# ScalarE's normalisation and routing pieces moved from the end of a pair slot into its middle, in a one-core attention and mixture-of-experts kernel

## The chip, the cores and the metric

The kernel runs on one core of a Trainium2 chip. The metric is the device time of one execution in microseconds (us). Before the change the median of three runs is 1081.94 us (1081.14 to 1083.57).

## What is computed

The input is x, 8 batches of 512 tokens with 128 features, and a conditioning vector per batch. Cut to what matters:

```python
h = layernorm(x) * (1 + ca) + sa
x = x + ga * attention(h, W_qkv, W_out)        # 16 heads of 64, rotary, causal mask, softmax
h = layernorm(x) * (1 + cb) + sb
x = x + gb * moe(h)                            # 8 experts, top 2, gelu, then a layernorm and + h
```

The router takes the two largest of eight logits, the expert's input rows are gathered by expert, and the residual inside the expert block is added afterwards.

## The kernel before, in words

**Stages.** A short opening (some 30 us) loads the data and prepares batches 0 and 1. Then comes the attention stage, which lasts to about 810 us and also does the routing of each finished batch. After it come the last routing pieces, the expert stage and a closing stage.

**The attention stage is a hand-written pipeline.** A *pair* is two heads of one batch; there are 64 of them, 8 per batch. The stage is a loop over 68 *slots*, numbered by step i (0 to 8) and c (0 to 7); slot (i, c) is number 8i + c. In one slot the engines work on three pairs at once: q0, whose q and k are projected, rotated and rounded to a high and a low part; q1, whose scores are computed, masked and exponentiated; and q2, whose exponentials are finished and transposed, multiplied with the values and projected. Every engine has its own instruction queue, written out in a fixed order by `pe_slot`, `act_slot`, `dve_slot`, `pool_slot` and `sp_slot` (lines 950 to 1218), and waits on semaphores for the others. Each engine starts a slot when it has finished the one before.

**TensorE's order in a slot** (`pe_slot`, line 950): the six projection matmuls of q0 (lines 852 to 859), the transposes "0" and "2a" of q2 (line 915), the scores of q1 of tile row 3 (lines 889 to 894), further transposes, the values of q2 (line 937), transposes "3a" of q1, more scores, the output projection of q2 (line 946), transposes "3b", the value projection (lines 873 to 875), then in slots c = 0, 2, 4, 6, 7 a routing or normalisation piece in PSUM bank 6, then the last scores. `pe_scores` of tile row 3 has to wait for the sixth exponential of q2 (unit 5), because that frees its PSUM banks:

```python
if due(NU * n + 2 * idx - 2):
    e.wait_ge(a_exp, NU * n + 2 * idx - 2)
```

**ScalarE's order in a slot** (`act_slot`, line 1043): exponentials 5, 6, 7 of q2; copies of transposes "0" and "2a"; `act_rep`; copy of "1"; `act_r`; exponentials 0 to 3 of q1 (line 996, the first waits for VectorE's maximum, `nmax`); the copy of "3a"; `act_hi` twice (line 1024, the rounding of k and of q, each of which waits for GpSimd's sum at line 1173); `act_v` (line 1028); exponential 4 of q1; and at the very end `route_act`. So what `route_act` does stands between exponential 4 and exponential 5 of the same pair.

**The side work** of step i belongs to other batches than the attention of that step:

- `n_rows`, `n_turn`, `n_features`, `n_rest` prepare batch i + 2 (steps 0 to 5): normalise the four token tiles of 128 x 128 (line 559), transpose them on TensorE (line 566), shift and scale into `ht2` (line 573) and round to `h_hi` (line 576) on ScalarE, and take the low part `h_lo` on GpSimd (line 581).
- `r_norm`, `r_features`, `r_shift` normalise the finished batch i - 1 (line 288, four tiles), transpose (line 295) and shift (line 303). The factors for it come from GpSimd's `r_factors` at the end of slot 5.
- `r_exp` (line 350), `r_rows` (line 314) and VectorE's `r_one` and others route batch i - 2.

Before the change ScalarE has `r_exp` at the end of slot 1, `r_rows` at the end of slot 2, `n_rows` at the end of slot 3, `n_features` with the rounding at the end of slot 4, `r_norm` at the end of slot 6 and `r_shift` at the end of slot 7. GpSimd takes `n_rest` at the start of slot 5, and waits there for the rounding.

**GpSimd's order in a slot** (`pool_slot`, line 1180): `route_rest`, `route_cum`, `pool_wo`, a wait for VectorE's `ot` of q2 (not in slot 0), `pool_qk` twice, `pool_lo` twice, `route_pool`. `pool_qk` also waits for four small transfers on SP's queue, which swap the halves of the heads for the rotation (line 1199). The first SP issue of a slot waits for VectorE's product at line 1075.

The side work that is left at the end of the 68 slots is walked through in `LATE` (line 1329), slots (8, 4) to (10, 1), with no attention beside it.

Of the kernel before, what the change touches and what calls it, by code (L numbers as in the profile page):

```python
# [13 lines left out]
B, S, E = 8, 512, 128  # L14
NT = B * S // P
TB = S // P
# [7 lines left out]
FIRST = 2  # L24
# [18 lines left out]
def due(value):  # L43

    return not isinstance(value, int) or value > 0
# [13 lines left out]
def adaln_kernel(nc, x_in, w_qkv, w_out, gate_w, expert_bias, w_up, w_down, c_t, w_mod,  # L59
                 cos_in, sin_in, ident_in, tri_in, rank_in, const_in, out, xs, ys):  # L60
    ctx = ExitStack()
    with ctx:
# [215 lines left out]
            e.wait_ge(r_rs, b + 1)  # L278
            e.tensor_tensor(minus, less, rstd4, op=ALU.mult).then_inc(r_fac, 1)

        def r_norm(e, b):
            e.wait_ge(r_fac, b + 1)
            if due(b - 1):
                e.wait_ge(d_xs, 16 * 2 * TB * (b - 1))
                e.wait_ge(d_h2, 16 * (b - 1))
            e.wait_ge(n_tr, min(b + 2, B - FIRST))
            for t in range(TB):
                ins = e.activation(rows[b % 2][:, t, 0:E], x_all[:, b * TB + t, :], ACT.Identity, bias=f4[:, 5, t:t + 1],
                                   scale=f4[:, 4, t:t + 1])
            ins.then_inc(r_xh, 1)  # L290

        def r_features(e, b):
            e.wait_ge(r_xh, b + 1)
# [184 lines left out]
        def route_pe(e, i, c):  # L478
# [9 lines left out]
            if c == 7 and a is not None:  # L488
                r_features(e, a)

        def route_act(e, i, c):
            b, a = batch(i, 2), batch(i, 1)
            if c == 1 and b is not None:
                r_exp(e, b)
            if c == 2 and b is not None:
                r_rows(e, b)
            if c == 3 and coming(i) is not None:
                n_rows(e, i, coming(i))
            if c == 4 and coming(i) is not None:
                n_features(e, i, coming(i))  # L500
            if c == 6 and a is not None:
                r_norm(e, a)
            if c == 7 and a is not None:
                r_shift(e, a)

# [43 lines left out]
            e.scalar_tensor_tensor(out=minus1[:, n], in0=mean[:, n], scalar=-1.0, in1=rstd[:, n],  # L549
                                   op0=ALU.mult, op1=ALU.mult).then_inc(n_fac, 1)  # L550

        def n_rows(e, i, b):
            e.wait_ge(n_fac, 1)
            if due(i - 2):
                e.wait_ge(d_xs, 16 * 2 * TB * (i - 2))
                e.wait_ge(d_h2, 16 * (i - 2))
            for t in range(TB):
                m = b * TB + t
                ins = e.activation(rows[(i + 1) % 2][:, t, 0:E], x_all[:, m, :], ACT.Identity,
                                   bias=minus1[:, m:m + 1], scale=rstd[:, m:m + 1])  # L560
            ins.then_inc(n_xh, 1)

        def n_turn(e, i):
            e.wait_ge(n_xh, i + 1)
# [4 lines left out]
        def n_features(e, i, b):  # L569
            e.wait_ge(n_tr, i + 1)  # L570
            if due(i - 1):
                e.wait_ge(p_x2, i - 1)
            e.activation(ht2[:], ps[:, BANK_R, :], ACT.Identity, bias=mod1[:, 0, b:b + 1],
                         scale=mod1[:, 1, b:b + 1]).then_inc(n_ht, 1)
            e.wait_ge(n_ht, i + 1)
            e.copy(h_hi[:, b * S:(b + 1) * S], ht2[:]).then_inc(n_hi, 1)

# [3 lines left out]
            e.tensor_tensor(h_lo[:, cols], ht2[:], h_hi[:, cols], op=ALU.subtract).then_inc(n_lo, 1)  # L581

        def route_rest(e, i, c):
            if c == 5 and coming(i) is not None:
                n_rest(e, i, coming(i))

        def route_cum(e, i, c):
# [207 lines left out]
        with ExitStack() as ph:  # L795
# [247 lines left out]
            def act_slot(e, i, c):  # L1043
                (q0, q1, q2), v = pairs(i, c), Tile(8 * i + c)
                if q2.live:
                    act_exp(e, q2, 5)
                    act_exp(e, q2, 6)
                    act_exp(e, q2, 7)
                    act_store(e, q2, "0")
                    act_store(e, q2, "2a")  # L1050
                    act_rep(e, q2)
                    act_store(e, q2, "1")
                    act_r(e, q2)
                if q1.live:
                    act_exp(e, q1, 0)
                    act_exp(e, q1, 1)
                    act_exp(e, q1, 2)
                    act_exp(e, q1, 3)
                    act_store(e, q1, "3a")
                if q0.live:  # L1060
                    act_hi(e, q0, 1)
                    act_hi(e, q0, 0)
                if v.live:
                    act_v(e, v)
                if q1.live:
                    act_exp(e, q1, 4)
                route_act(e, i, c)
# [111 lines left out]

            def pool_slot(e, i, c):  # L1180
                q0, _, q2 = pairs(i, c)
                route_rest(e, i, c)
                route_cum(e, i, c)
                if q2.live:
                    pool_wo(e, q2)
                if q0.live:
                    if q2.live and i and c:

                        e.wait_ge(v_ot, q2.n + 1)
                    pool_qk(e, q0, 1)  # L1190
                    pool_qk(e, q0, 0)
                    pool_lo(e, q0, 1)
                    pool_lo(e, q0, 0)
                route_pool(e, i, c)

            def sp_turn(e, q):
# [65 lines left out]
        with ExitStack() as ph:  # L1262
# [194 lines left out]
            with nc.Block() as block:  # L1457
# [50 lines left out]
                def _(e):  # L1508
                    high(e, 0)
                    high(e, 1)  # L1510
                    for i, c in LATE:
                        route_act(e, i, c)
                        if (i, c) == (B + 1, 0):
                            e.wait_ge(s_gb, 1)
                            e.copy(gb[:].rearrange("p b f -> p (b f)"),
                                   ps[:, 0:2, :].rearrange("p b f -> p (b f)")).then_inc(s_gbc, 1)
# [212 lines left out]
```

## Time and profile before

| | |
|---|---|
| median of three runs | 1081.94 us |
| the profiled execution's own time | 1080.8 us |
| its span, first to last instruction | 1078.9 us |
| busy: TensorE / VectorE / ScalarE / GpSimd | 86% / 79% / 68% / 52% of the span |
| mean granted TensorE clock | 0.953 |

The span is cut into stretches by the start of the k projection of each slot (line 852), which TensorE issues first in every slot; what is called "the stretch of slot (i, c)" runs from there to the next such start. In a timeline a row gives the start, the duration, the engine, line and operation, and in brackets how long the engine had been idle before and what released it. Rows of ScalarE overlap by about 0.1 us where one follows the other at once, so the distance of starts is the time that an instruction takes of the queue.

### The profile page before, as it was taken

The page shows a single profiled execution, that of the slowest core. Times are in us where ns is not written, and L with a number is a line of the kernel's source. Part 1 is how long each engine was busy: PE and PEld are TensorE (multiplying, and loading weights), DVE is VectorE, ACT ScalarE, POOL GpSimd, SP SyncE. Part 2 cuts the span into 40 slices and gives each one's busy share as a digit, 9 for nine tenths or more (in the row PEclk, how much of TensorE's full clock was granted, in tenths as well). Part 3 has the DMA queues.
Part 4 walks back from the last instruction along what each step waited for, and adds up shares of the span by engine and source line. Part 5 has one row for each costly group of instructions (what it writes and reads, how often), then busy time and mean ns, then how long its engine had stood idle before and what let it go on. Part 6 is the DMA issues. An engine that isn't in the chain of part 4 may idle for free. (4 is left out here: it accounts for less than half of the span.)

```text
span 1078.9 us, 20269 instructions
## 1 busy us (share of the span) xinstructions
PE 927.0 (86%) x6154; PEld 666.3 (62%) x6154; DVE 847.5 (79%) x1731; ACT 730.2 (68%) x1927; POOL 557.8 (52%) x634
## 2 busy tenths in 40 slices
PE   4599999999999999999999999999996179999800
PEld 2366666666666667667666667666664167888600
DVE  5478888788878888888888888788876569988627
ACT  2278777778777777877777777777774256667504
POOL 1245446444665557465556646564673606766610
PEclk9999999999999999999999999999998579999955
DMA  7222322232222222222322232223122756676334
GB/s 241 53 50 50 74 50 50 50 73 61 50 64 72 60 64 69 60 53 73 79 50 50 64 85 57 56 74 77 45 60 97 237 195 244 244 238 236 126 104 130
DMA packets 67227, 104.27 MB, mean 97 GB/s; under 512 B 11115, under 2 KB 49912, under 8 KB 63536
## 3 DMA queue, kind: packets, MB, share of 16 engines
q1 hardware_dynamic: 59056, 90.53, 29.2%
q0 software_dynamic: 4992, 8.94, 2.8%
q10 hardware_dynamic: 3072, 3.51, 0.9%
q8 instruction: 52, 0.85, 0.3%
q14 instruction: 55, 0.45, 0.1%
HBM read 21.09 MB, written 15.50 MB: 34 GB/s over the span
## 5 line engine op out<-in xcount | busy, mean ns | idle before, releaser
L1173 POOL TENSOR_TENSOR four<-four 128x512 f32<-128x512 f32 x128 | 161.2, 1281 | 334.5 <-DVE ot L1119 213.8
L996 ACT ACTIVATE prob<-ps,nmax 128x512 f32<-128x512 f32 (+3 forms) x512 | 264.5, 529 | 76.1 <-DVE nmax L1096 76.1
L1096 DVE TENSOR_REDUCE nmax<-ps 128x2 f32<-128x1024 f32 (+3 forms) x256 | 211.0, 824 | 8.8
L915 PE MATMUL ps<-ident,prob 128*128 128x128 f32 x1280 | 191.4, 279 | 12.2 <-ACT probt L1017 6.9
L915 PEld LDWEIGHTS ps<-ident,prob 128*128 128x128 f32 x1280 | 142.2, 141 | 62.5 <-ACT prob L996 36.7
L1177 POOL TENSOR_TENSOR qk_lo<-four,qk_hi 128x512 fp32r<-128x512 f32 x128 | 162.3, 1291 | 0.0
L937 PE MATMUL ps<-probt,val 128*64 128x512 f32 (+3 forms) x1024 | 153.6, 442 | 0.2 <-ACT probt L1017 0.2
L1089 DVE TENSOR_TENSOR ps<-ps,tri 128x256 f32<-128x256 f32 x256 | 109.3, 427 | 53.5 <-PE ps L894 52.7
L1024 ACT CAST qk_hi<-four 128x512 fp32r<-128x512 f32 x128 | 79.5, 621 | 96.7 <-POOL four L1173 96.7
L1017 ACT COPY probt<-ps 128x512 f32<-128x512 f32 (+2 forms) x256 | 124.7, 520 | 19.6 <-PE ps L915 19.6
L1585 POOL DMA_INDIRECT results<-y,to_i x92 | 96.6, 1050 | 73.0 <-DVE y L1429 50.7
L889 PE MATMUL ps<-qk_hi 64*128 64x512 f32 (+3 forms) x256 | 105.0, 410 | 17.3 <-ACT prob L996 16.5
L937 PEld LDWEIGHTS ps<-probt,val 128*64 128x64 f32 x1024 | 68.3, 137 | 74.8 <-issue 60.6
L1075 DVE TENSOR_TENSOR four<-ps,turn_s 128x1024 f32<-128x1024 f32 x64 | 78.4, 1224 | 42.7 <-PE ps L859 42.7
L890 PE MATMUL ps<-qk_hi 64*128 64x512 f32 (+3 forms) x256 | 105.6, 413 | 0.0
L996 ACT ACTIVATION_READ_ACCUMULATOR prob<-ps,nmax 128x1 f32 x512 | 105.0, 205 | 0.0
L889 PEld LDWEIGHTS ps<-qk_hi 64*128 64x128 f32 x256 | 47.2, 185 | 66.6 <-issue 54.6
L1526 ACT ACTIVATE hf<-ps 128x512 f32<-128x512 f32 x92 | 55.2, 601 | 45.5 <-PE ps L1373 45.1
L894 PE MATMUL ps<-qk_lo,qk_hi 64*128 64x512 f32 (+3 forms) x256 | 82.1, 321 | 0.0
L892 PE MATMUL ps<-qk_hi,qk_lo 64*128 64x512 f32 (+3 forms) x256 | 82.0, 320 | 0.0
L893 PE MATMUL ps<-qk_lo,qk_hi 64*128 64x512 f32 (+3 forms) x256 | 82.0, 320 | 0.0
L891 PE MATMUL ps<-qk_hi,qk_lo 64*128 64x512 f32 (+3 forms) x256 | 82.0, 320 | 0.0
(222 smaller groups left out, 2163.4 us busy)
## 6 DMA issues: line engine op xcount, KB each, us to landing
four<-four SPq DMA_DIRECT2D x256, 128.0 KB
wt<-wall SPq DMA_DIRECT2D x23, 1024.0 KB, 4.8
xg<-slots SPq DMA_DIRECT2D x23, 288.0 KB, 3.8
hb<-h_hi SPq DMA_DIRECT2D x64, 64.0 KB, 2.1
hb<-h_lo SPq DMA_DIRECT2D x64, 64.0 KB, 2.0
y<-results SPq DMA_DIRECT2D x8, 512.0 KB, 7.3
x_all<-in_x SPq DMA_DIRECT2D x4, 512.0 KB, 10.6
h_hi<-rows SPq DMA_DIRECT2D x8, 256.0 KB, 2.7
```

Of the source, the lines that this page charges most:

```text
L889: e.matmul(o0, hi[top_, 0, cols], hi[top_, 1, 0:w], start=True, stop=False)
L890: e.matmul(o1, hi[low_, 0, cols], hi[low_, 1, 0:w], start=True, stop=False)
L894: e.matmul(o1, hi[low_, 0, cols], lo[low_, 1, 0:w], start=False, stop=True).then_inc(p_s, 1)
L915: mm = e.transpose(ps[:, PT + at % 2, at_block * P:(at_block + 1) * P], prob[:, unit, kk * P:(kk + 1) * P], ident[:])
L937: mm = e.matmul(ps[j * HD:(j + 1) * HD, W0, kk * P:S], v[:, kk, first + j * HD:first + (j + 1) * HD], probt[q.par][:, j, kk, kk * P:S], st ...
L996: e.activation(prob[:, unit, 0:w], ps[:, bank_s(idx) + j, 0:w], ACT.Exp, bias=nmax[:, q.par, idx, j:j + 1], accum_out=den[:, q.par, 2 * i ...
L1017: e.copy(dst, src).then_inc(a_ev, 1)
L1089: e.tensor_tensor(block_, block_, tri[:].unsqueeze(1).to_broadcast([P, 2, P]), op=ALU.add).then_inc(v_tri, 1)
L1096: e.tensor_reduce(nmax[:, q.par, idx, :], ps[:, bank:bank + 2, 0:w], AX.X, ALU.max, negate=True).then_inc(v_max, 1)
L1173: e.tensor_tensor(qk[:, cols], tt[:, cols], ur[:, cols], op=ALU.add).then_inc(g_qk, 1)
L1177: e.tensor_tensor(qk_lo[q.par][:, half, :], qk[:, half * S:(half + 1) * S], qk_hi[q.par][:, half, :], op=ALU.subtract).then_inc(g_lo, 1)
L1585: e.indirect_dma_start(ys, bass.IndirectOffsetOnAxis(to_i[:, j % 4, t:t + 1], 0), y4[:, j % 2, t, :], None, bounds_check=2 * B * S - 1, oo ...
```

## The change

The pieces that read no PSUM bank are taken out of `route_act` into a new `route_act_part(e, i, c, half)`, called twice in a ScalarE slot: with half 0 in front of the first exponential of q1, and with half 1 behind the copy of "3a" and in front of `act_hi`. `r_norm` and `n_rows` do two tiles in each half, and stand a slot later than before (slots 7 and 4). `r_exp` goes from the end of slot 1 to half 0 of slot 2. The rounding to `h_hi` is parted from `n_features` as `n_high` and goes from the end of slot 4 to half 0 of slot 5. GpSimd's `n_rest` goes from the start of slot 5 to slot 6, behind `pool_lo`. `r_rows`, the shift of `n_features` and `r_shift` stay at the end of slots 2, 4 and 7. TensorE's, VectorE's and SP's orders are as before.

```diff
-        def r_norm(e, b):
-            e.wait_ge(r_fac, b + 1)
-            if due(b - 1):
-                e.wait_ge(d_xs, 16 * 2 * TB * (b - 1))
-                e.wait_ge(d_h2, 16 * (b - 1))
-            e.wait_ge(n_tr, min(b + 2, B - FIRST))
-            for t in range(TB):
+        def r_norm(e, b, half):
+            if half == 0:
+                e.wait_ge(r_fac, b + 1)
+                if due(b - 1):
+                    e.wait_ge(d_xs, 16 * 2 * TB * (b - 1))
+                    e.wait_ge(d_h2, 16 * (b - 1))
+                e.wait_ge(n_tr, min(b + 2, B - FIRST))
+            for t in range(2 * half, 2 * half + 2):
                 ins = e.activation(rows[b % 2][:, t, 0:E], x_all[:, b * TB + t, :], ACT.Identity, bias=f4[:, 5, t:t + 1],
                                    scale=f4[:, 4, t:t + 1])
-            ins.then_inc(r_xh, 1)
+            if half:
+                ins.then_inc(r_xh, 1)
...
+        def route_act_part(e, i, c, half):
+
+            b, a = batch(i, 2), batch(i, 1)
+            if c == 2 and half == 0 and b is not None:
+                r_exp(e, b)
+            if c == 4 and coming(i) is not None:
+                n_rows(e, i, coming(i), half)
+            if c == 5 and half == 0 and coming(i) is not None:
+                n_high(e, i, coming(i))
+            if c == 7 and a is not None:
+                r_norm(e, a, half)
+
         def route_act(e, i, c):
             b, a = batch(i, 2), batch(i, 1)
-            if c == 1 and b is not None:
-                r_exp(e, b)
             if c == 2 and b is not None:
                 r_rows(e, b)
-            if c == 3 and coming(i) is not None:
-                n_rows(e, i, coming(i))
             if c == 4 and coming(i) is not None:
                 n_features(e, i, coming(i))
-            if c == 6 and a is not None:
-                r_norm(e, a)
             if c == 7 and a is not None:
                 r_shift(e, a)
...
             e.activation(ht2[:], ps[:, BANK_R, :], ACT.Identity, bias=mod1[:, 0, b:b + 1],
                          scale=mod1[:, 1, b:b + 1]).then_inc(n_ht, 1)
+
+        def n_high(e, i, b):
             e.wait_ge(n_ht, i + 1)
             e.copy(h_hi[:, b * S:(b + 1) * S], ht2[:]).then_inc(n_hi, 1)
...
         def route_rest(e, i, c):
-            if c == 5 and coming(i) is not None:
+            if c == 6 and coming(i) is not None:
                 n_rest(e, i, coming(i))
...
                     act_r(e, q2)
+                route_act_part(e, i, c, 0)
                 if q1.live:
                     act_exp(e, q1, 0)
                     act_exp(e, q1, 1)
                     act_exp(e, q1, 2)
                     act_exp(e, q1, 3)
                     act_store(e, q1, "3a")
+                route_act_part(e, i, c, 1)
                 if q0.live:
                     act_hi(e, q0, 1)
                     act_hi(e, q0, 0)
...
             def pool_slot(e, i, c):
                 q0, _, q2 = pairs(i, c)
-                route_rest(e, i, c)
                 route_cum(e, i, c)
...
                     pool_lo(e, q0, 0)
+                route_rest(e, i, c)
                 route_pool(e, i, c)
```

`n_rows` is split in the same way as `r_norm`, and in the `LATE` loop both halves of `route_act_part` stand in front of `route_act`.

## Rows read from the trace of the kernel before

**Rows 1.** The page, part 2: busy tenths of TensorE in 40 equal slices

```profile
PE   4599999999999999999999999999996179999800
```

**Rows 2.** Busy time by stretch: slots (4, 1) and (6, 4), no piece ahead of them

```profile
core 0: us, PE busy (x) PEld busy (x) DVE busy (x) ACT busy (x) POOL busy (x), PEclk, DMA share, GB/s
640.18:651.50 11.32, 11.32 (x83) 7.84 (x81) 10.13 (x20) 8.63 (x26) 5.42 (x6) 1.00 0.25 60
...
408.93:420.21 11.28, 11.28 (x84) 7.91 (x82) 9.88 (x18) 8.41 (x25) 7.96 (x9) 1.00 0.30 80
```

**Rows 3.** The same view: slot 4 behind n_rows, step 4, and six steps' sum

```profile
443.72:457.01 13.29, 11.88 (x88) 8.40 (x86) 10.23 (x20) 10.74 (x32) 6.02 (x6) 1.00 0.22 51
...
sum 79.26, PE 71.50 PEld 50.35 DVE 60.84 ACT 64.38 POOL 35.09; mean PE 11.92 PEld 8.39 DVE 10.14 ACT 10.73 POOL 5.85
```

**Rows 4.** The same view: slot 5 behind n_features, step 4, and six steps' sum

```profile
457.01:469.07 12.06, 11.43 (x84) 7.93 (x82) 10.37 (x20) 9.31 (x27) 6.09 (x7) 1.00 0.23 54
...
sum 72.27, PE 68.60 PEld 47.63 DVE 61.48 ACT 55.13 POOL 35.71; mean PE 11.43 PEld 7.94 DVE 10.25 ACT 9.19 POOL 5.95
```

**Rows 5.** The same view: slot 7 behind r_norm, step 3, and seven steps' sum

```profile
383.54:396.64 13.10, 11.86 (x88) 8.43 (x86) 10.23 (x19) 10.47 (x30) 5.75 (x6) 1.00 0.22 51
...
sum 93.37, PE 83.60 PEld 58.84 DVE 71.99 ACT 74.66 POOL 41.77; mean PE 11.94 PEld 8.41 DVE 10.28 ACT 10.67 POOL 5.97
```

**Rows 6.** The same view: slots (4, 0) behind r_shift, (4, 3) behind r_rows

```profile
396.64:408.93 12.29, 12.15 (x92) 8.88 (x90) 9.90 (x17) 9.42 (x28) 7.63 (x8) 1.00 0.23 67
...
432.06:443.72 11.66, 11.48 (x83) 7.80 (x81) 10.29 (x21) 8.97 (x26) 5.29 (x6) 1.00 0.32 80
```

**Rows 7.** Timeline of TensorE in slot (3, 7)

```profile
386.77 0.46 PE L889 MATMUL ps<-qk_hi 64*128 64x512 f32 x1 [1.04 <-ACT prob L996]
...
395.56 0.60 PE L295 MATMUL ps<-ident,rows 128*128 128x128 f32 x4
396.09 0.38 PE L889 MATMUL ps<-qk_hi 64*128 64x256 f32 x1
```

**Rows 8.** Timeline of ScalarE in slot (3, 7) and the start of (4, 0)

```profile
384.43 1.64 ACT L288 ACTIVATE rows<-x_all,f 128x128 f32<-128x128 f32 x4
385.97 0.56 ACT L996 ACTIVATE prob<-ps,nmax 128x384 f32<-128x384 f32 x1
...
391.02 0.69 ACT L996 ACTIVATE prob<-ps,nmax 128x512 f32<-128x512 f32 x1 [0.96 <-DVE nmax L1096]
...
394.39 0.62 ACT L1024 CAST qk_hi<-four 128x512 fp32r<-128x512 f32 x1 [0.75 <-POOL four L1173]
395.64 0.62 ACT L1024 CAST qk_hi<-four 128x512 fp32r<-128x512 f32 x1 [0.63 <-POOL four L1173]
...
397.87 0.59 ACT L996 ACTIVATE prob<-ps,nmax 128x384 f32<-128x384 f32 x1
```

**Rows 9.** Timeline of ScalarE at the start of slots (4, 2) and (4, 5)

```profile
421.11 0.23 ACT L350 ACTIVATE expo<-first 128x32 f32<-128x32 f32 x1
...
457.48 0.78 ACT L573 ACTIVATE ht<-ps,mod 128x512 f32<-128x512 f32 x1
458.30 0.62 ACT L576 CAST h_hi<-ht 128x512 fp32r<-128x512 f32 x1
458.82 0.58 ACT L996 ACTIVATE prob<-ps,nmax 128x384 f32<-128x384 f32 x1
```

**Rows 10.** Timeline of GpSimd in slots (3, 7) and (4, 5)

```profile
385.27 0.46 POOL L1164 TENSOR_TENSOR wog<-wo,ga 128x128 f32<-128x128 f32 x1
393.08 2.53 POOL L1173 TENSOR_TENSOR four<-four 128x512 f32<-128x512 f32 x2 [7.35 <-DVE ot L1119]
...
458.99 1.30 POOL L581 TENSOR_TENSOR h_lo<-ht,h_hi 128x512 fp32r<-128x512 f32 x1 [0.63 <-ACT h_hi L576]
```

**Rows 11.** Timelines of GpSimd and of TensorE around slot (1, 7)

```profile
183.82 2.52 POOL L1173 TENSOR_TENSOR four<-four 128x512 f32<-128x512 f32 x2 [2.30 <-DMA four<-four]
...
187.53 0.50 PE L857 MATMUL ps<-h_hi,wq_hi 128*128 128x512 f32 x1 [0.39 <-ACT val L1028]
```

More of the change, by code:

```diff
@@ L550, in n_factors, with n_rows @@
                                    op0=ALU.mult, op1=ALU.mult).then_inc(n_fac, 1)
[L552 to L557, printed above, removed]
+        def n_rows(e, i, b, half):
+            if half == 0:
+                e.wait_ge(n_fac, 1)
+                if due(i - 2):
+                    e.wait_ge(d_xs, 16 * 2 * TB * (i - 2))
+                    e.wait_ge(d_h2, 16 * (i - 2))
+            for t in range(2 * half, 2 * half + 2):
                 m = b * TB + t
@@ L560, in n_rows @@
                                    bias=minus1[:, m:m + 1], scale=rstd[:, m:m + 1])
-            ins.then_inc(n_xh, 1)
+            if half:
+                ins.then_inc(n_xh, 1)
         def n_turn(e, i):
@@ L1511, in _ @@
                     for i, c in LATE:
+                        route_act_part(e, i, c, 0)
+                        route_act_part(e, i, c, 1)
                         route_act(e, i, c)
```

## The prediction

> **What bounds the kernel now.** I read the page's slices first [rows 1]. TensorE shows 9 in every slice of the attention stage, so that stage, three quarters of the time, goes at TensorE's pace, and a slot can become shorter only where TensorE idles. Next I cut the stage into its slots [rows 2]. A slot with no ScalarE piece ahead of it, and no routing work on TensorE, takes 11.28 us (slot (4, 1)) or 11.32 us (slot (6, 4)), and TensorE is busy in all of it. In other slots two things are added: TensorE's own side work, and idle time. Side work: four transposes start at 395.56 and the next scores at 396.09, so they cost 0.53 us [rows 7]. The rest is waiting. Slot 4 takes 13.29 us, of which TensorE is busy 11.88 [rows 3]; slot 5 takes 12.06, busy 11.43 [rows 4]; slot 7 takes 13.10, busy 11.86 [rows 5].
>
> What TensorE waits for is in its timeline [rows 7]: in slot (3, 7) the first scores start at 386.77 after 1.04 us of idleness, released by an exponential. ScalarE's timeline says why [rows 8]: exponential 5, which frees the scores' banks, starts at 385.97, 2.43 us into the slot, directly behind the four tiles of `r_norm`, which were started at 384.43. The four tiles take 1.54 us of the queue (385.97 less 384.43), and exponential 5 itself waits for nothing: no idle time stands before it. Without the tiles it starts 0.89 us into the slot. Where only the 0.78 us shift `r_shift` lies ahead, exponential 5 starts at 397.87, 1.23 us into slot (4, 0), and TensorE idles 0.14 us (12.29 less 12.15); behind `r_rows` it idles 0.18 [rows 6, 8]. So up to about 1.1 us into the slot an exponential 5 is free, and later it costs TensorE its lateness.
>
> ScalarE has room elsewhere in the same slot: 0.96 us of idleness before the first exponential, for VectorE's maximum, then 0.75 us before the first `act_hi` and 0.63 us before the second, both for GpSimd [rows 8].
>
> **The change part by part.**
>
> *n_rows leaves the end of slot 3 (6 steps).* The six slots 4 take 79.26 us together [rows 3]. Without the stall each should be a plain slot 4 plus the four transposes, 11.32 + 0.53 = 11.85 us [rows 2, 7], six times 71.1. I leave 0.3 us for step 1, whose exponentials are already late by another cause. Gain 79.26 - 71.4 = 7.9 us.
>
> *The rounding leaves the end of slot 4 (6 steps).* The shift stays. In step 4 exponential 5 starts at 458.82, 1.81 us into slot 5; the shift started at 457.48 and takes about 0.7 us of the queue, so it would start 1.15 us in [rows 9], close to slot (4, 0). I leave 0.2 us of waiting, a little over the 0.14 and 0.18 of [rows 6]. Six slots of 11.28 + 0.20 are 68.9 us, against 72.27 [rows 4]: gain 3.4 us.
>
> *r_norm leaves the end of slot 6 (7 steps; the eighth runs behind the attention, in the same order as before, gain 0).* The seven slots 7 take 93.37 us [rows 5]; seven of 11.28 + 0.53 are 82.7. In step 1, and as I judge by its length in one other step, a transfer lands late: GpSimd waits for it at 183.82, ScalarE's copy of the values is late, and TensorE's projection waits 0.39 us for that [rows 11]. This stays; I put 1.2 us for both. Gain 93.37 - 83.9 = 9.5 us.
>
> *r_exp goes to slot 2.* It takes 0.12 us of the queue (0.23 less the overlap) ahead of a slot that hardly stalls [rows 9]. Between 0 and 0.7 us over six steps; I take 0.2, near the lower end, since exponential 5 starts within the free 1.1 us in most steps.
>
> *Where the pieces arrive.* Two tiles take 0.77 us of the queue with neighbours close behind, 0.87 with none (half of 1.54, plus the 0.10 by which instructions overlap). In front of the first exponential there are 0.96 idle us [rows 8], and with the overlap behind `act_r` a little over 1.0: covered, and `r_exp` and the rounding (458.82 less 458.30, 0.52 us [rows 9]) all the more. In front of `act_hi` there are 0.75 us, so the first rounding may be 0.1 us late; but the second waits another 0.63 us for GpSimd's second sum, which doesn't depend on the first rounding, and `act_v` and exponentials 4 and 5 queue behind that second one. Price 0 as long as the lateness stays below 0.63 us. The added waits (the factors, the scatter of an older batch, TensorE's transposes) were all met long before. Behind half 1 TensorE waits for the last tile: half 1 would end near 394.4 in the times of slot (3, 7), and `r_features` starts at 395.56 [rows 7, 8], over 1 us to spare. VectorE's `r_one` waits for `r_exp`, which ScalarE now runs while it waits for VectorE's maximum; VectorE reaches `r_one` only after that maximum.
>
> The nearest rule speaks of small instructions. The Trainium skill (Perfetto Trace Analysis, Optimizing Scalar/DVE Operations) gives ScalarE some 93 ns of data access per instruction on SBUF, beyond its work, and counsels grouping where the engine is saturated. By that rule 26 separated pieces would lose that each, 2.4 us if it all showed, and the time would be 1063.3; the rows have the loss inside an idle gap, so my sum leaves it out.
>
> *n_rest on GpSimd.* It takes 1.30 us [rows 10] and goes from the start of slot 5, where GpSimd idled for the rounding, to the end of slot 6's work: where it runs on at 385.27 with `pool_wo` and then idles 7.35 us for VectorE. That idleness hides it; bare it would cost 6 x 1.3 = 7.8 us. `r_cum`, `r_factors` and the scatters keep their places or are passed by nothing. `r_shift` waits for it, and comes some 10 us later. SP's loads of batch i + 2 need it only in step i + 2. No DMA moves.
>
> **The sum.** 7.9 + 3.4 + 9.5 + 0.2 = 21.0 us. The profiled execution took 1080.8 us, so 1059.8; the median of the runs is 1.1 us over it, so 1060.9 us. Stages after the attention are unchanged. TensorE's idle time alone (79.26 - 71.50, 72.27 - 68.60, 93.37 - 83.60) sums to 21.2 us [rows 3 to 5], before what I leave as waiting: the same size.
>
> **The rivals.**
>
> *B, the gaps are too small.* Each half that overflows its gap delays the first exponentials or, past 0.63 us, the second rounding. With 0.3 us for each of 26 halves 7.8 us are given back: 1068.7. For it: the pieces fill 0.87 of 0.96 and 0.75 us, with semaphore waits still to be served. Against it: the second rounding's 0.63 us.
>
> *C, the transfer becomes the wait.* A slot that is 1.3 us shorter leaves the rotation's swap less time before GpSimd needs it. In slot (1, 6) it landed late and TensorE stood 0.39 us [rows 11]. If all 13 shortened slots lose 0.6 us, again 7.8 us: 1068.7. Against it: in slot (3, 7) GpSimd waits for VectorE, not for the transfer [rows 10], and most slots behave so.
>
> *D, the stall stays, 1081.9.* That needs exponential 5 to be held by something else; it had no idle time of its own [rows 8].
>
> *E, slower.* ScalarE itself is the pace of the middle of the slot, so that its idle gaps are only the echo of the stall at the slot's head and vanish with it. Then all moved time is paid: 13 x 1.54 + 6 x 0.52 + 7 x 0.12 = 24.0 us against 21.0 won, 1084. It decides where more than 87% of the moved time shows. Against it: the gaps are there also in slots that don't stall, where TensorE is busy throughout and ScalarE only 8.41 of 11.28 us [rows 2].
>
> **How the numbers follow.** Forecast 0.77, B 0.09, C 0.06, D 0.03, E 0.05. About 0.2% is what a measurement can tell from no change, so faster 0.92, same 0.04, slower 0.04 (E lies just at that edge). The predicted time is 1061.0. Downwards, no waiting left in slot 5 (1.2 us) and the late landings gone (1.2, and more in slots I don't count) give 1057. Upwards the range takes in B and C: 1070.
>
> **What would show it.** Right: slots 4 and 7 at about 11.85 us, slot 5 near 11.5; exponential 5 about 1 us into slots 4 and 7; TensorE's 1.04 us before the first scores gone; ScalarE idle about 0.1 us before the first exponential in slots 4 and 7, and still some 0.6 before the second `act_hi`; GpSimd's low part within slot 7's idle time. Wrong: first exponentials later than VectorE's maximum, GpSimd waiting for transfers in slots 4 and 7, or slots 4 and 7 above 12.3 us.

## The result and the profile after

The changed kernel takes 1063.91 us (median of four runs, 1060.71 to 1068.13), the kernel before 1082.76 us (1081.14 to 1084.12). The ratio is 0.9845, interval 0.9823 to 0.9866: 18.9 us faster, where 21.0 were forecast; the median lies 2.9 us over the predicted time, inside the range. The profiled execution of the changed kernel is the longest of the four, 1068.13 us with a span of 1066.2, so stretches are compared rather than spans. From the first k projection to the last it takes 744.4 us (35.5 to 779.8), against 762.3 before (32.1 to 794.4): 17.9 us gained. Ahead of that it is 3.3 us longer, behind it 1.9 (286.4 against 284.5). The 3.3 us are no part of the change: a second profile of the same kernel (experiment *after_again*) has its first k projection at 32.05 and 743.0 us of attention; the tail is 287.2 us there, which stays open below.

The page of the changed kernel, its costliest group and the busiest DMA queue (before: 334.5 us of idleness ahead of that group, 29.2% on the queue):

```profile
PE   3499999999999999999999999999995189999800
...
q1 hardware_dynamic: 59056, 90.53, 29.8%
...
L1187 POOL TENSOR_TENSOR four<-four 128x512 f32<-128x512 f32 x128 | 161.3, 1282 | 320.2 <-DVE ot L1133 169.9
```

The windows of slots (4, 4), (4, 5) and (3, 7), which answer to [rows 3 to 5], each with the sum of the same six or seven steps. Columns are those of [rows 2]: length, then busy time of TensorE, its weight loads, VectorE, ScalarE and GpSimd.

```profile
436.63:448.39 11.76, 11.76 (x88) 8.34 (x86) 10.13 (x20) 10.51 (x31) 5.87 (x6) 1.00 0.24 58
...
sum 70.63, PE 70.63 PEld 50.02 DVE 60.21 ACT 63.10 POOL 34.01; mean PE 11.77 PEld 8.34 DVE 10.04 ACT 10.52 POOL 5.67
...
448.39:459.94 11.55, 11.39 (x83) 7.80 (x81) 10.36 (x20) 9.34 (x27) 4.95 (x6) 1.00 0.24 57
...
sum 69.37, PE 68.40 PEld 46.97 DVE 61.28 ACT 54.55 POOL 27.78; mean PE 11.40 PEld 7.83 DVE 10.21 ACT 9.09 POOL 4.63
...
376.91:388.62 11.71, 11.71 (x87) 8.40 (x85) 10.15 (x19) 9.95 (x29) 6.45 (x7) 1.00 0.25 57
...
sum 83.27, PE 82.53 PEld 58.63 DVE 71.37 ACT 71.56 POOL 44.60; mean PE 11.79 PEld 8.38 DVE 10.20 ACT 10.22 POOL 6.37
```

Slots 4 went from 79.26 to 70.63 us (gain 8.6), slots 5 from 72.27 to 69.37 (2.9), slots 7 from 93.37 to 83.27 (10.1). That is 21.6 us, a little over the forecast. TensorE is busy in all of slots 4, and idles 0.74 us in the seven slots 7 together. What is missing is found in a slot that no term of the sum named, slot 0 (steps 2 to 8; first the kernel before, then the changed one):

```profile
sum 85.42, PE 84.54 PEld 61.62 DVE 69.23 ACT 69.24 POOL 56.01; mean PE 12.08 PEld 8.80 DVE 9.89 ACT 9.89 POOL 8.00
```

```profile
388.62:401.51 12.89, 12.44 (x92) 8.77 (x90) 9.96 (x17) 10.69 (x31) 9.33 (x9) 1.00 0.26 64
...
sum 88.33, PE 86.08 PEld 61.16 DVE 69.60 ACT 72.43 POOL 60.09; mean PE 12.30 PEld 8.74 DVE 9.94 ACT 10.35 POOL 8.58
```

Slot (4, 0) took 12.29 us before [rows 6] and takes 12.89; the seven together are 2.9 us longer.

ScalarE's timeline of slot (3, 7) and the start of (4, 0), against [rows 8]:

```profile
377.83 0.58 ACT L1008 ACTIVATE prob<-ps,nmax 128x384 f32<-128x384 f32 x1
...
381.92 0.89 ACT L289 ACTIVATE rows<-x_all,f 128x128 f32<-128x128 f32 x2
383.19 0.69 ACT L1008 ACTIVATE prob<-ps,nmax 128x512 f32<-128x512 f32 x1 [0.39 <-DVE nmax L1110]
...
385.69 0.90 ACT L289 ACTIVATE rows<-x_all,f 128x128 f32<-128x128 f32 x2
386.98 0.62 ACT L1036 CAST qk_hi<-four 128x512 fp32r<-128x512 f32 x1 [0.39 <-POOL four L1187]
388.22 0.62 ACT L1036 CAST qk_hi<-four 128x512 fp32r<-128x512 f32 x1 [0.62 <-POOL four L1187]
...
389.80 0.78 ACT L305 ACTIVATE ht<-ps,modt 128x512 f32<-128x512 f32 x1
390.46 0.59 ACT L1008 ACTIVATE prob<-ps,nmax 128x384 f32<-128x384 f32 x1
```

Exponential 5 starts 0.92 us into slot (3, 7) (2.43 before), both halves of `r_norm` fit their gaps with 0.39 us to spare, and the 0.62 us ahead of the second `act_hi` are still there. But exponential 5 of slot (4, 0) starts 1.84 us in, against 1.23. The half of `r_norm` in front of `act_hi` is not what made it late here, since ScalarE waits 0.39 us for GpSimd behind it. GpSimd's timeline, and TensorE's at the place where it stops:

```profile
378.68 1.31 POOL L593 TENSOR_TENSOR h_lo<-ht,h_hi 128x512 fp32r<-128x512 f32 x1
379.94 0.47 POOL L1178 TENSOR_TENSOR wog<-wo,ga 128x128 f32<-128x128 f32 x1
385.67 2.52 POOL L1187 TENSOR_TENSOR four<-four 128x512 f32<-128x512 f32 x2 [5.26 <-DMA four<-four]
...
390.63 0.76 PE L927 MATMUL ps<-ident,prob 128*128 128x128 f32 x5 [0.28 <-ACT ht L305]
```

`n_rest` (378.68) lies in GpSimd's idle time, as forecast. The sum of the rotation's halves, though, waits for the swap's transfer, 8.76 us into the slot, where [rows 10] had it waiting for VectorE. And VectorE itself has `r_slots` (0.62 us from 383.87 to 384.49) directly ahead of `ot`, with no idleness anywhere near:

```profile
383.53 0.42 DVE L1110 TENSOR_REDUCE nmax<-ps 128x2 f32<-128x256 f32 x1
383.87 0.22 DVE L447 TENSOR_TENSOR at<-hot,share 128x64 f32<-128x64 f32 x1
...
384.49 0.69 DVE L1133 TENSOR_TENSOR ot<-ps,rs 128x512 f32<-128x512 f32 x1
```

So two suspects stand for the loss behind slot 7: the late swap, and VectorE's routing piece. The swap is the last to arrive in four of the seven slots 7, (1, 7), (3, 7), (4, 7) and (7, 7), and the slots 0 behind these lost 0.42, 0.60, 0.53 and 1.00 us, the other three 0.03 to 0.19. In the kernel before it was last in none of the seven. GpSimd's waits ahead of that sum, over the whole kernel (us in total, times, longest), of before and then of after:

```profile
POOL four L1173 <- DVE ot L1119: 213.8, 41, 7.6
POOL four L1173 <- DMA four<-four: 120.7, 23, 18.5
```

```profile
POOL four L1187 <- DVE ot L1133: 169.9, 35, 7.9
POOL four L1187 <- DMA four<-four: 150.3, 29, 18.5
```

Together they are 64. The transfer came last in 23 of them, and in 29 now (26 in the second profile of the change). Eight of these are slots 0, where GpSimd does not wait for `ot` at all, and six belong to step 0.

### The profile page after: what moved, and what is told of

Read it like the earlier page. It is cut to its first block and busy times, and to the rows that moved or that the text cites. A ratio compares the mean times of both kernels' runs of the same rounds, so it can differ in the third digit from the quotient of the medians.

```text
span 1066.2 us, 20269 instructions
## 1 busy us (share of the span) xinstructions
PE 926.3 (87%) x6154; PEld 665.3 (62%) x6154; DVE 845.8 (79%) x1731; ACT 729.9 (68%) x1927; POOL 558.1 (52%) x634
## 5 line engine op out<-in xcount | busy, mean ns | idle before, releaser
L1125 DVE COPY probt<-ps 128x512 f32<-128x512 f32 (+1 forms) x128 | 78.6, 614 | 2.8 <-PE ps L927 2.8
## 6 DMA issues: line engine op xcount, KB each, us to landing
x_all<-in_x SPq DMA_DIRECT2D x4, 512.0 KB, 10.1
```

## The experiments

Twelve runs were made, on two chips. On one of them the kernel before takes 1095.08 us (beside the first four runs below) and 1089.34 us (beside the next four), on the other 1082.40. On the slower chip all profiles have a longer tail, 290 to 297 us behind the last k projection against 284 to 287. The kernel before was timed there, and not profiled again, so ratios are of one chip, and sums of slots are set against the first profiles. Each run has one profile, and in it a single slot can be 1 or 2 us longer than the others of its kind; where that matters the regular ones are named.

### One part of the change at a time

*only_norm*, *only_rows* and *only_high* each make one of the three moves; the other pieces are called at their old places.

```diff
 def route_act_part(e, i, c, half):
     b, a = batch(i, 2), batch(i, 1)
     if c == 7 and a is not None:          # only_norm
         r_norm(e, a, half)
...
     if c == 4 and coming(i) is not None:  # only_rows
         n_rows(e, i, coming(i), half)
...
     if c == 5 and half == 0 and coming(i) is not None:  # only_high, with n_rest
         n_high(e, i, coming(i))
```

> Only r_norm is moved (slot 7, two tiles in each half); n_rows, the rounding, n_rest and r_exp stand where they stood before. My theory (each move returns its own stall; the change's lengthened slots 0 come from the rotation's swap landing late in the shortened slot 7): the seven slots 7 sum to 83.3 us as in the change (before 93.4), slots 4 and 5 stay at 79.3 and 72.3 us, the seven slots 0 (steps 2 to 8) sum to about 88 us as in the change (before 85.4): some 7.5 us less than before, 1075. Rival (slots 0 are late because of n_rows, n_rest or the rounding, or by chance): slots 0 stay at 85.4 and the time is 1072.5.

Measured: 1088.52 us, ratio 0.9939 (0.9916 to 0.9962). Slots 7 take 83.53 us (9.8 gained), slots 0 88.43:

```profile
sum 88.43, PE 86.19 PEld 61.19 DVE 69.58 ACT 72.92 POOL 60.97; mean PE 12.31 PEld 8.74 DVE 9.94 ACT 10.42 POOL 8.71
```

The 3.0 us of slots 0 come with this one move, and not with the sum of the moves. Slots 5 stay (72.40), but slots 4 take 81.47 us, 2.2 more than before, mostly in one slot of 15.34 us, for which no run gives a cause.

> Only n_rows is moved (slot 4, two tiles in each half). Theory: the six slots 4 sum to 70.7 us (before 79.3), slots 5 about 72.3, slots 0 about 85.4 as before, slots 7 93.4: 8.6 us less than before, 1074. Rival (a late swap in the shortened slot 4 hurts the slot behind it as it does behind slot 7): slots 5 sum to over 74 us and the gain is under 7 us.

Measured: 1086.49 us, ratio 0.9914 (0.9885 to 0.9943). Slots 4 take 71.11 us (8.2 gained). Slots 5, which this kernel doesn't touch, take 74.17 us, 1.9 more than before. That much the rival had forecast, though not a gain under 7 us: it is 8.6. In slot (4, 5) exponential 5 starts at 454.10, 1.92 us in (before: 1.81), and TensorE idles 0.53 us for it; two slots of the six are 12.45 and 13.07 us, and in front of the longer one, in slot (3, 4), GpSimd's sum was released by the transfer. So a slot 4 that has become shorter hands a part on, as slot 7 does. With the rounding moved as well (the change) slots 5 are 69.37 us.

> Only the rounding to h_hi (slot 5, half 0) and GpSimd's low part (slot 6, behind pool_lo) are moved. Theory: the six slots 5 sum to 69.4 us (before 72.3), all other kinds as before; 3 us less, 1079.7. Rival (n_rest behind pool_lo is in the way of slot 7's pool_wo or of SP's transfers): slots 7 grow by some 0.3 us each, 2 us in sum, and the gain shrinks to 1 us.

Measured: 1092.62 us, ratio 0.9978 (0.9957 to 0.9999). Slots 5 take 68.57 us, 3.7 gained, a little more than forecast, and in five of the six TensorE waits no more than 0.06 us. Slots 7 are not longer (92.34), so the rival is out. The three ratios give 0.61 + 0.86 + 0.22 = 1.69%, the whole change gave 1.55% and later 1.72%: the parts add up within the intervals.

### Is it the swap?

*short_swap* is the changed kernel with a quarter of the columns in each transfer of the swap, except the first. It leaves the other three quarters of each swap out, so that stale values enter the rotation.

```diff
-e.dma_start(ur[to:to + 32, :], uu[frm:frm + 32, :]).then_inc(d_ur, 16)
+w = 2 * S if q.n == 0 else S // 2
+e.dma_start(ur[to:to + 32, 0:w], uu[frm:frm + 32, 0:w]).then_inc(d_ur, 16)
```

> The change, but from the second pair on each of the four swap transfers for the rotation moves a quarter of its columns (the rest of the rotated values is stale, so q and k are not the reference's); the number of transfers, semaphores and issues is the same. Theory (a late landing of the swap is what lengthens slots 0 and single other slots): GpSimd waits for VectorE and not for the transfers in slots 1 to 7, the seven slots 0 (steps 2 to 8) sum to about 86 us (88.3 in the change), slots 2 of steps 3 and 6 fall from 13.0 to 11.85, and the time is 4 to 5 us less than the change's 1063.9. Rival (half 1 of r_norm in front of act_hi is what makes slot 0 late): slots 0 stay at 88 us and the time falls by less than 2.5 us.

Measured: 1068.16 us, ratio 0.9759 (0.9735 to 0.9783), attention 739.4 us, 5.0 and 3.6 less than in the two profiles of the change. Slots 0 take 86.84 us; the row is slot (4, 0):

```profile
382.88:395.34 12.46, 12.29 (x91) 8.84 (x89) 9.97 (x17) 10.13 (x30) 9.28 (x10) 1.00 0.13 35
...
sum 86.84, PE 85.36 PEld 61.32 DVE 69.57 ACT 71.25 POOL 61.93; mean PE 12.19 PEld 8.76 DVE 9.94 ACT 10.18 POOL 8.85
```

About half of the 2.9 us goes with the transfer's size; 1.4 are left. Of these 0.8 are in slots (2, 0) and (8, 0), behind two slots 7 in which the smaller transfer still came last. The other 0.6 are in slots (4, 0) to (7, 0), of which two take a regular 12.46 us in place of 12.29 and 12.26, with GpSimd released by VectorE in the slot 7 ahead: there the second suspect is at work. Slots (3, 2) and (6, 2), which were to fall to 11.85 us, take 12.15 and 12.16 (12.95 and 13.14 in the first profile of the change; 12.40 and 12.18 in the second), so those slots are not explained by the transfer's size.

### Is it VectorE's routing piece?

*slots_last* puts `r_slots` at the end of VectorE's slot 7.

```diff
-            if c == 7:
-                r_slots(e, b)
...
+            if c == 7 and b is not None:
+                r_slots(e, b)
```

> The change with VectorE's r_slots (three small instructions, 0.6 us in slot 7) taken from in front of ot to the end of VectorE's slot 7. Theory (beside the late swap, slot 0 is lengthened because r_slots makes ot 0.3 us late in the slot that no longer stalls, and GpSimd, the roundings, exponential 4 and r_shift follow): ot starts 7.3 us into slots 7 (7.57 in the change), slots 0 fall by 0.15 to 0.2 us each, some 1.3 us less than the change. Rival (only the swap's landing): slots 0 as in the change, time the same.

Measured: 1074.11 us, ratio 0.9851 (0.9813 to 0.9890), attention 750.9. `ot` does come 0.30 us earlier, 7.28 us into slot (3, 7), and slots 0 are nonetheless 91.40 us, 3.1 longer than the change's. VectorE's timeline at the border of slots (3, 7) and (4, 0), which starts at 388.75:

```profile
388.18 1.28 DVE L447 TENSOR_TENSOR at<-hot,share 128x64 f32<-128x64 f32 x1
389.50 0.22 DVE L449 TENSOR_REDUCE at<-at 128x8 f32<-128x64 f32 x1
389.75 0.91 DVE L453 CAST slot_of<-at 128x8 int32<-128x8 f32 x1
390.57 0.42 DVE L1103 TENSOR_TENSOR ps<-ps,tri 128x256 f32<-128x256 f32 x1
...
sum 91.40, PE 86.06 PEld 61.38 DVE 76.34 ACT 70.57 POOL 58.31; mean PE 12.29 PEld 8.77 DVE 10.91 ACT 10.08 POOL 8.33
```

The same three instructions now take 2.4 us in place of 0.62: the first and the third each end when one of the two passes of GpSimd's `pool_lo` ends (they start at 388.10 and take 2.53 us together, so about 389.4 and 390.6). VectorE's mask of the next slot starts at 390.57, 1.82 us in, where the change has it 0.11 in. The expectation failed because it priced `r_slots` at its old duration. It neither clears nor convicts the piece; that comes with *two_swaps*.

### One gap instead of two

*half0* does all four tiles in front of the first exponential, *half1* all four in front of `act_hi`.

```diff
-for t in range(2 * half, 2 * half + 2):
+for t in range(4 if half == 0 else 0):    # half1: range(4 if half else 0)
```

> The change with all four tiles of n_rows and r_norm in half 0, in front of the first exponential, none in half 1. Theory (the idle time there is 1.06 us with the overlap, and four tiles take 1.54): the first exponential comes 0.5 us late in slots 4 and 7, TensorE waits for it at the transposes 3a, slots 4 and 7 grow by about 0.3 us each, 4 us more than the change. Rival (the first exponential has slack of its own): slots 4 stay at 11.76 and slots 7 at 11.72 us.

> The change with all four tiles in half 1, in front of act_hi, none in half 0. Theory (0.75 us idle there and 0.63 us behind the first rounding take up 1.54 us nearly whole): slots 4 and 7 as in the change within 0.05 us, the second rounding at most 0.1 us later, time within 1.5 us of the change. Rival (the first rounding decides, since GpSimd's low part waits for it): slots 0 and 5 grow by 0.7 us each, 9 us more than the change.

Measured: *half0* 1073.51 us, ratio 0.9854 (0.9811 to 0.9897); *half1* 1072.40 us, 0.9852 (0.9812 to 0.9893). Regular slots 4 and 7 of *half0* are 12.02 and 12.00 us where the change has 11.76 and 11.71, and in slots 7 of *half1* 11.96. In front of the first exponential four tiles thus cost 0.26 to 0.29 us a slot more than two and two, some 3.6 us over 13 slots; in front of `act_hi` they cost 0.25 in slots 7 and up to 0.17 in slots 4. In *half0* a part comes back in slots 0:

```profile
sum 84.93, PE 84.39 PEld 61.80 DVE 69.22 ACT 66.93 POOL 53.61; mean PE 12.06 PEld 8.83 DVE 9.89 ACT 9.56 POOL 7.66
```

That row (slots 0 of *half0*) is 3.4 us less than the change's: the slots 0 behind its longer slots 7 lose nothing.

*half1* shows that the length of slot 7 alone doesn't decide it. Its slots 7 are as long, 11.96 us, and its slots 0 take 88.65 us all the same. ScalarE's queue in its slot (6, 7), which starts at 660.31, has no wait left in front of either rounding:

```profile
669.32 1.67 ACT L289 ACTIVATE rows<-x_all,f 128x128 f32<-128x128 f32 x4
670.87 1.14 ACT L1036 CAST qk_hi<-four 128x512 fp32r<-128x512 f32 x2
671.90 0.59 ACT L1040 COPY val<-ps 128x512 f32<-128x512 f32 x1
```

`act_v` starts 11.59 us into the slot, where the change has 11.41, and what follows is later by the same 0.18 us. So neither expectation of *half1* held: slots 7 grew by 0.25 us, and slots 0 and 5 by 0.3 and 0.7 us in sum, not each. The attention takes 746.3 and 746.6 us in the two, 743.0 to 744.4 in the change; the ratios don't tell the three apart.

### Fewer or other transfers

*swap_act* gives two of the swap's four transfers to ScalarE's queue, behind its first two copies of q2.

```diff
-for to, frm in ((0, 32), (32, 0), (64, 96), (96, 64)):   # SP
+for to, frm in ((0, 32), (32, 0)):                       # SP
...
+def act_turn(e, q):                                      # ScalarE
+    e.wait_ge(v_u, q.n + 1)
+    for to, frm in ((64, 96), (96, 64)):
+        e.dma_start(ur[to:to + 32, :], uu[frm:frm + 32, :]).then_inc(d_ur, 16)
```

> The change with two of the four swap transfers issued from ScalarE's queue, behind the copy of transposes 2a, instead of SP's. Theory (late landings lengthen single slots; SP needs 2.46 us to issue four): the swaps land 1 us earlier, GpSimd waits for them less often, slots 0 fall to the 86.8 us of the run with short swaps, 2 us less than the change, provided that an issue takes little of ScalarE's time. Rival (each issue holds ScalarE 0.6 us as it does SP): the copy of transposes 1 comes 1.2 us late in every slot and TensorE stalls, over 20 us more than the change.

Measured: 1117.41 us, ratio 1.0242 (1.0210 to 1.0273). ScalarE's own queue shows the two issues and what they cost the engine:

```profile
397.85 1.16 ACTq L1034 DMA_DIRECT2D four<-four  x2
399.10 0.62 ACT L1057 COPY rrep<-rden 128x512 f32<-128x512 f32 x1 [1.24 <-issue]
```

The rival held. The attention takes 792.2 us, 47.8 more than in the change: 0.45 us more in each slot 0, 0.9 in each slot 7 and 1.0 in each slot 4. Slots 7 are alike now (12.76 to 12.79 us), and the transfer comes last in only 14 of GpSimd's waits, but each slot pays more than the late landings had cost.

*two_swaps* turns the four transfers of 32 partitions into two of 64: the halves of a head's rotation are interleaved instead of stacked (the order of the weights' columns and of the tables is changed to match), and a transfer takes every second partition.

```diff
-for to, frm in ((0, 32), (32, 0), (64, 96), (96, 64)):
-    e.dma_start(ur[to:to + 32, :], uu[frm:frm + 32, :]).then_inc(d_ur, 16)
+for k in range(2):
+    e.dma_start(ur[k:P:2, :], uu[1 - k:P:2, :]).then_inc(d_ur, 16)
...
-e.wait_ge(d_ur, 64 * n + 64)
+e.wait_ge(d_ur, 32 * n + 32)
...
-order = np.concatenate([np.arange(0, HD, 2), np.arange(1, HD, 2)])
+order = np.arange(HD)
...
-"cos": for_qk(np.concatenate([co, co], 0)),
-"sin": for_qk(np.concatenate([si, -si], 0)),
+"cos": for_qk(np.stack([co, co], 1).reshape(HD, S)),
+"sin": for_qk(np.stack([si, -si], 1).reshape(HD, S)),
```

*before_two_swaps* is the kernel before with the same edit, *after_again* the changed kernel as it is, for a comparison on one chip.

> The change with the two halves of each rotation interleaved on the partitions (the columns of q and k weights and the tables reordered before the launch), so that the swap is two transfers of 64 partitions, every second one, in place of four of 32; the bytes are the same. Theory (SP's four issues of 0.6 us put the last landing late, and late landings cost the change some 5 us): the swap lands 1.2 us earlier, GpSimd waits for VectorE in nearly all slots, slots 0 (steps 2 to 8) sum to about 86.8 us, and the time is 4 to 6 us less than the change's. Rival (a transfer of twice the rows takes as long as two to issue and land): time within 1.5 us of the change, GpSimd's waits for the transfers as many as before.

> The kernel before with the same two interleaved transfers. Theory (the stalled slots hid part of the late landings, so the kernel before gains less from early ones than the change does): 2 to 4 us less than the kernel before; the stalls of slots 4 (79.3), 5 (72.3) and 7 (93) stay. Rival (late landings cost both kernels the same): it gains as much as the change does from the same edit.

> The change itself, beside the other three of this call on one chip. Theory: its ratio to the kernel before is again 0.984 (some 17 us less), the slots as in its first profile: slots 4, 5 and 7 sum to 70.6, 69.4 and 83.3 us, slots 0 to over 87 us (85.4 before). Rival (the lengthening of slots 0 was one profile's accident): slots 0 sum to under 86.5 us.

Measured, the kernel before at 1082.40 us:

| | median us | ratio | attention us | slots 0 | slots 7 | GpSimd's waits for the swap |
|---|---|---|---|---|---|---|
| after_again | 1063.62 | 0.9828 (0.9806 to 0.9850) | 743.0 | 88.08 | 83.74 | 26, 134.7 us |
| two_swaps | 1055.22 | 0.9752 (0.9738 to 0.9766) | 735.7 | 86.23 | 82.72 | 16, 73.4 us |
| before_two_swaps | 1073.64 | 0.9924 (0.9907 to 0.9940) | 754.9 | 85.37 | 92.00 | 15, 69.8 us |

*two_swaps* beats both kernels, by 27.2 and 8.4 us (4 to 6 less than the change were expected). SP's issue and GpSimd's sum in its slot (4, 0), which starts at 380.59:

```profile
383.53 1.10 SPq L1213 DMA_DIRECT2D four<-four  x2
```

```profile
386.99 2.52 POOL L1187 TENSOR_TENSOR four<-four 128x512 f32<-128x512 f32 x2 [1.75 <-DMA four<-four]
```

In the kernel before, SP needs more than twice as long for the same data, and in slot (3, 7) of the changed kernel it needed 3.67 us (the second fence), after which the landing was the late one seen above. A long issue is not the whole of it: in slots (1, 7), (4, 7) and (7, 7) the landing was late behind issues of 2.46 to 2.47 us.

```profile
386.48 2.46 SPq L1199 DMA_DIRECT2D four<-four  x4
```

```profile
379.86 3.67 SPq L1213 DMA_DIRECT2D four<-four  x4
```

The edit is worth as much to the kernel before (8.8 us of the median, 7.4 of the attention) as to the changed one (8.4 and 7.2 beside *after_again*), as the rival of *before_two_swaps* had it. So the change did not make late landings dearer in sum; it moved where they fall. That a slot with a stall hides a landing that a short one shows fits this, but single profiles scatter too much to show it slot by slot. And with the landings out of the way in both, slots 0 still differ by 86.23 - 85.37 = 0.86 us, 0.14 to 0.19 in each of slots (4, 0) to (8, 0), as in the regular slots of *short_swap*. Slots (2, 0) and (3, 0) lose nothing (12.19 against 12.18, 12.27 against 12.28), and they say what the loss needs. Slot (1, 7) is 11.72 us long, with both halves of `r_norm` in their new places, but `r_slots` doesn't run yet in step 1. These are VectorE's `ot` in slot (1, 7), which starts at 180.41, and in slot (3, 7), which starts at 368.87, of *two_swaps*:

```profile
187.69 0.69 DVE L1133 TENSOR_TENSOR ot<-ps,rs 128x512 f32<-128x512 f32 x1 [0.24 <-PE ps L949]
```

```profile
376.33 0.17 DVE L453 CAST slot_of<-at 128x8 int32<-128x8 f32 x1
376.44 0.69 DVE L1133 TENSOR_TENSOR ot<-ps,rs 128x512 f32<-128x512 f32 x1
```

`ot` starts 7.28 us into the one and 7.57 into the other, and the slots 0 behind them:

```profile
192.13:204.32 12.19, 12.16 (x91) 8.92 (x90) 9.88 (x17) 9.85 (x29) 6.97 (x8) 1.00 0.15 55
...
380.59:393.05 12.46, 12.29 (x92) 8.84 (x90) 9.97 (x17) 10.13 (x30) 9.26 (x10) 1.00 0.19 66
```

In step 2 `r_slots` does run, but slot (2, 7) is 12.30 us long, and slot (3, 0) loses nothing. So the loss appears where slot 7 is short and `r_slots` stands ahead of `ot`; `r_norm`'s half in front of `act_hi` alone doesn't make it. This is a comparison of slots that also differ in other routing pieces, and one slot has to stand for the case without `r_slots`; the run meant to show it bare (*slots_last*) put a larger cost beside it.

### n_rest

*rest_early* calls `n_rest` again at the start of GpSimd's slot 5.

```diff
-            if c == 6 and coming(i) is not None:
+            if c == 5 and coming(i) is not None:
                 n_rest(e, i, coming(i))
...
+                route_rest(e, i, c)
                 route_cum(e, i, c)
...
-                route_rest(e, i, c)
                 route_pool(e, i, c)
```

> The change with GpSimd's n_rest back at the start of slot 5, where it must now wait for the rounding that ScalarE does in front of the first exponential of that slot. Theory (the rounding ends about 6.4 us into slot 5, n_rest and pool_wo 8.3 us into it, which is when VectorE's ot frees GpSimd): slots 5 and 6 grow by at most 0.1 us each, time within 1 us of the change. Rival (pool_wo is late for the output projection): slots 5 grow by 0.3 us or more each, 2 us more than the change.

Measured: 1064.85 us, ratio 0.9831 (0.9815 to 0.9847); the change on the same chip has 0.9828. Slots 5 take 70.54 us, 1.5 more than in *after_again*, but regular ones 11.53 us as there, with two single ones of 12.00 and 12.51; other slots are shorter and the attention takes 743.0 us in both. The new place is worth nothing that can be measured, and costs nothing.

## Why the prediction was right, and where it was not

**n_rows, r_norm:** right in place and size. 8.6 and 10.1 us in the first profile, 8.1 and 9.6 in the second, against 7.9 and 9.5. Exponential 5 is released 0.92 us into slot 7, and TensorE's 1.04 us [rows 7] are gone: the first scores start at 379.05 with no idleness ahead. Each of the two moves alone brings its own gain.

**The rounding:** 2.9 and 3.3 us against 3.4; alone 3.7. The 0.2 us of waiting that were left for the shift show as 0.16 (11.55 less 11.39).

**r_exp:** its 0.2 us can't be seen. It was not moved alone, and regular slots 2 take 11.84 to 11.86 us before and after.

**The arrival in the gaps:** right for ScalarE. Both halves fit, with 0.39 us to spare each, and *half0* and *half1* show the price had they not been parted, up to 0.29 us a slot. Rival B, that the gaps are too small, is out, and so is E: ScalarE's gaps were no echo of the stall. (E's time should have been 1084.9 by its own terms, 1060.9 + 24.0, and not 1084.) The Trainium skill's overhead per instruction (Perfetto Trace Analysis, Optimizing Scalar/DVE Operations), 2.4 us by the prediction's estimate, doesn't show: slots 4 are 11.76 us with TensorE busy throughout, so what ScalarE lost on separated pieces lay in its idle time.

The forecast stands in time and mechanism. **The step that failed** in it is the pricing of all that follows a shortened slot at nothing. The sum ended at slots 4, 5 and 7, and the only transfer cost in it was the one already seen in [rows 11]. In fact slots 0 are 2.9 us longer in the first profile and 2.7 in the second. Shown for it: it comes with `r_norm`'s move alone (*only_norm*), goes where slot 7 is 0.3 us longer and nothing else is late (*half0*; not in *half1*), and splits in two, late landings of the swap (2.0 us by *two_swaps*, 1.5 by *short_swap*) and a regular 0.86 us that follows VectorE's `r_slots` by the comparison above. The first is rival C's mechanism at a quarter of its price: it was given 7.8 us on 13 slots, and what shows is 2 us, behind slots 7. The second was in nobody's list.

Against C the prediction had put that in slot (3, 7) GpSimd waits for VectorE, not for the transfer [rows 10]. That was so in all seven slots 7, but it says who is last, not by how much, and `ot` was last because the stall had delayed it too. Where the transfer was last in the kernel before, GpSimd's sum started 4.3 to 6.5 us after the swap's first issue. In slots 7 `ot` released it 6.3 to 6.9 us after that issue, behind nearly all of this range. With the stall gone `ot` releases it 5.4 us after the issue (slots (2, 7), (5, 7) and (6, 7)), and 13 of the 23 were later than that. The range could have been read from the trace before.

The books: 21.6 us gained in slots 4, 5 and 7, 2.9 lost in slots 0, 0.8 lost in all other slots (not traced to a cause), so 17.9. The three gains were forecast at 20.8 us together; that they came out 0.8 us larger in this profile hides a part of the step that failed, and in the second profile they are 21.0. **Open:** the tail behind the attention is 1.9 and 2.7 us longer in the two profiles of the change, 1.8 in *rest_early*, and not at all in *two_swaps* (284.4 us). No run was made for that, and on the other chip tails scatter by 7 us.

## What to carry to other kernels

A piece of work that reads no shared buffer can be moved into waits of its own engine, in portions as large as each wait, and its whole cost at the old place comes back. But ask of the slot that becomes shorter what its length had been hiding. It isn't enough to see who is the last to arrive: compare when the last one will come after the change with the whole range of times at which the next one has come, over all slots, since one slot's timeline shows only one. And where a transfer is nearly late, fewer issues for the same bytes can be worth nearly half as much (8.4 us beside 18.8).

## What the runs showed of the hardware

- One issue of a 128 KB transfer between partitions holds the issuing queue for about 0.6 us (four: 2.46 us in most slots of the changed kernel, up to 3.92; two on ScalarE's queue: 1.16 us, with the engine idle for 1.24), and two of twice the partitions take 1.10. ScalarE pays that with computing time.
- A landing scatters. Where the transfer came last, GpSimd's sum starts 4.3 to 6.6 us after the swap's first issue in the changed kernel (5.8 in slot (3, 7), 385.67 less 379.86), and 3.0 to 5.8 us after it in *two_swaps* (3.5 in slot (4, 0), 386.99 less 383.53).
- Beside the two-operand differences of GpSimd's `pool_lo` VectorE's product of 128x64 took 1.28 us in place of 0.22 and its cast of 128x8 0.91 in place of 0.17, while its reduction between them kept its 0.22. The Trainium skill (SBUF — State Buffer, SBUF: two separate sides) has VectorE and GpSimd share one port pair that one instruction holds to its end, for VectorE only where it reads two SBUF operands or is in a two-port mode. The trace of *slots_last* agrees for two of the three: the product has two operands, the reduction one. The cast has one, and no trace shows in which mode it runs.
- TensorE's granted clock between 45 and 58 us was 0.50 (1.2 GHz) in the first profile of the change and 1.00 (2.4 GHz) in the second, of the same kernel; before that stretch TensorE had been busy 13.27 and 11.79 us of 30. First the one, then the other:

```profile
45.00:58.00 13.00, 7.55 (x31) 5.48 (x32) 6.09 (x10) 6.79 (x15) 6.98 (x7) 0.50 0.21 50
```

```profile
45.00:58.00 13.00, 10.19 (x46) 7.00 (x45) 7.86 (x12) 6.39 (x18) 5.89 (x6) 1.00 0.22 52
```

- The kernel before takes 1082.40 us on one chip and 1089 to 1095 on another. In the runs on the second, whatever the variant, 290 to 297 us lie behind the attention, in those on the first 284 to 287.
